# Channel mixing, sphere matrices and sphere convolution as one unrolled stage, ordered by batch entry

## The reference, cut to what matters

```python
x = x + L0_conv(_gn(x), ...)          # attention; its last step is a 1x1 convolution over channels
x = x + L1_conv(_gn(x), weight, bias) # sphere convolution

def _gn(v, G=4, eps=1e-05):           # per batch entry: mean and variance over 2 channels x 256 x 512
    ...
def _L1_conv_ref(x, weight, bias):
    gx, gy = compute_maps(H, W, 3, 3)  # where each of the 9 taps falls on the sphere, constant
    v = bilinear_sample(x, gx, gy)     # 4 neighbours per tap, columns wrap round
    y = einsum('bchwk,ock->bohw', v, w) + bias
```

## Time and profile before

| | |
|---|---|
| median of 3 runs | 1318.74 us (1318.55 to 1319.75) |
| profiled execution | 1318.1 us, span 1315.9 us |
| mean granted clock of TensorE | 0.946 of full |
| busy in the span | PE 1124.3 (85%), VectorE 965.2 (73%), ScalarE 655.0 (50%), GpSimd 820.7 (62%) |
| DMA | 159.28 MB, mean 121 GB/s |

### The profile page before, as it was taken

The page is one execution under the profiler, slowest core; times in us unless marked ns, Lnnn a source line. Parts: engine busy times, 40 slices in busy tenths (PEclk is TensorE's granted clock), DMA queues, the critical chain, the costliest instruction groups (busy, mean ns, idle before and its releaser), DMA issues. The chain is left out here.

```text
span 1315.9 us, 31260 instructions
## 1 busy us (share of the span) xinstructions
PE 1124.3 (85%) x12690; PEld 758.5 (58%) x12690; DVE 965.2 (73%) x1460; ACT 655.0 (50%) x1077; POOL 820.7 (62%) x689
## 2 busy tenths in 40 slices
PE   0399999999883888999999999999994986778997
PEld 0177777777660356666666666666673433434553
DVE  3789899999655998889998998998733881223434
ACT  1555555555430565656666666666662232223456
POOL 0467777777655698888898888888880002890000
PEclk9999999999995789999999999999897997979999
DMA  8824424433367428181717272520005985896621
GB/s 299 249 83 128 120 69 125 118 102 96 64 139 151 73 75 137 36 119 43 138 34 113 51 126 46 107 65 26 18 22 161 339 295 140 190 209 195 202 81 57
DMA packets 138189, 159.28 MB, mean 121 GB/s; under 512 B 19609, under 2 KB 87453, under 8 KB 138057
## 3 DMA queue, kind: packets, MB, share of 16 engines
q1 hardware_dynamic: 113592, 119.37, 38.4%
q10 hardware_dynamic: 15792, 28.81, 6.3%
q0 software_dynamic: 8672, 9.23, 3.3%
HBM read 106.48 MB, written 52.90 MB: 121 GB/s over the span
## 5 line engine op out<-in xcount | busy, mean ns | idle before, releaser
L1126 POOL TENSOR_TENSOR a_pl<-a_prob 128x512 bf16<-128x512 f32 x416 | 452.1, 1113 | 58.1 <-ACT a_prob L1083 54.1
L1083 ACT ACTIVATE a_prob<-a_col 128x512 f32<-128x512 f32 x512 | 303.1, 597 | 190.4 <-PE a_col L973 179.9
L1027 DVE TENSOR_REDUCE a_negmax<-a_row 128x1 f32<-128x512 f32 x512 | 336.9, 693 | 52.4 <-PE a_row L951 52.1
L990 PE MATMUL a_mix<-a_vp,a_prob 128*128 128x65 bf16 x2048 | 196.5, 195 | 1.1 <-DVE a_o L1052 0.9
L990 PEld LDWEIGHTS a_mix<-a_vp,a_prob 128*128 128x128 bf16 x2048 | 164.7, 99 | 54.1 <-issue 6.1
L991 PE MATMUL a_mix<-a_vp,a_pl 128*128 128x65 bf16 x2048 | 194.9, 195 | 0.0
L730 POOL TENSOR_TENSOR f_yl<-f_y,f_yh 128x768 bf16<-128x768 f32 x80 | 132.4, 1674 | 96.6 <-ACT f_yh L677 96.6
L991 PEld LDWEIGHTS a_mix<-a_vp,a_pl 128*128 128x128 bf16 x2048 | 147.5, 99 | 61.8 <-issue 6.3
L677 ACT ACTIVATE f_yh<-f_y 128x768 bf16<-128x768 f32 x80 | 67.4, 844 | 138.9 <-DVE f_y L568 119.7
L951 PE MATMUL a_row<-k,q 96*128 96x512 bf16 x256 | 109.1, 432 | 29.5 <-PEq L222 15.0
L1522 PE MATMUL s_acc<-s_xh,sphere_mat_h 128*104 128x512 bf16 x256 | 103.6, 405 | 35.3 <-DVE s_xl L1489 34.2
(11 more groups left out here) (151 smaller groups left out, 2308.5 us busy)
## 6 DMA issues: line engine op xcount, KB each, us to landing
X<-r_x ACTq DMA_DIRECT2D x16, 526.0 KB, 7.6
q<-in_x SPq DMA_DIRECT2D x8, 1024.0 KB, 7.8
a_v<-V SPq DMA_DIRECT2D x16, 512.0 KB, 4.5
Z<-a_z ACTq DMA_DIRECT2D x32, 256.0 KB, 2.8
r_z<-Z SPq DMA_DIRECT2D x16, 512.0 KB, 8.7
r_x<-in_x SPq DMA_DIRECT2D x32, 256.0 KB, 8.1
s_res<-X SPq DMA_DIRECT2D x38, 208.0 KB
out<-s_y ACTq DMA_DIRECT2D x38, 208.0 KB
```

The lines of the kernel that those rows point to most:

```text
L990: nc.tensor.matmul(mix[h % 2][:, qt, :], ph[p][:, kt, at], vpart, start=kt == 0, stop=False)
L1027: nc.vector.reduce_max(negmax[u][:, QT * h + qt:QT * h + qt + 1], row[row_buffer(h, qt)][:], AX.X, negate=True).then_inc(max_done, 1)
L1083: nc.scalar.activation(prob[head % PROBS][:, kt, :], col[kt % 2][:], ACT.Exp).then_inc(exp_done, 1)
L1126: nc.gpsimd.tensor_tensor(pl[head % PROBS][:, kt, :], prob[head % PROBS][:, kt, :], ph[head % PROBS][:, kt, :], ALU.subtract).then_inc(lo_ ...
```

## The change

`residual` and `sphere` become one function `blend` in one block, without loops: every instruction is written out with constant addresses and constant semaphore values.

- Batch entry 0 is mixed first (8 pairs); makes start with its third pair, two per pair, so 12 of them. Then entry 1's pairs alternate with the rest of the makes and with windows of entry 0: PE does `window(n - 2)` behind pair n, so windows 0 to 5 lie there. The last 4 makes follow, then the other windows.
- The order of windows is that of `places()`: per batch entry ten near windows, the three polar blocks, seven near windows; entry 0 whole, then entry 1.
- Statistics are finished per entry, and scale and offset stay in SBUF: the store and load of S are gone.
- Buffers: z, x and x1 of pairs three deep (four before); raw windows, residuals and y three deep each (one per batch entry before); xn, xh, xl and the window accumulators two deep.
- GpSimd waits until all X1 of an entry is stored, then makes the six copies and the 117 tile loads for this entry alone, entry 0 and then entry 1. The tiles lie in the space of q0 and k0, one set for both entries; a tile is reloaded when entry 0's step on it has been normalised. `normalise` waits for all of an entry's tile loads before its first polar step.
- SP issues the loads of 11 pairs, then per window one raw load, the residual of the window before, and one more pair while there are any. The first raw load of an entry waits for all its X1 stores.
- The last 2 of the weight parts' four subtractions move behind VectorE's first pair; PE waits for the parts before its first make and not before its first pair.

The diff, cut to the new lines that set the order and the buffers (removed lines are left out); the two functions that it removes are printed whole above, and operations not shown here (statistics, makes, wraps, activations) are those of before with other addresses.

```diff
...
+def blend(nc, T, Z, X1, XP, out, mixing, spaces):
...
+        U, RAWS, RES, TWO, ACCS = 3, 3, 3, 2, 3
...
+        MIDDLE = 10
...
+        res = [sb(f"b_res{s}", [M, W]) for s in range(RES)]
+        y = [sb(f"b_y{s}", [M, W]) for s in range(RES)]
+        held = [t[:].bitcast(FP32) for t in spaces]
+        fits = held[0].shape[1] // (W + 1)
+        polar = [held[t // fits][:, t % fits * (W + 1):(t % fits + 1) * (W + 1)] for t in range(TILES)]
...
+            around = [(m, None) for m in range(MIDDLE)] + [(None, m) for m in range(len(SPHERE_POLAR))] + [(m, None) for m in range(MIDDLE, NEARS)]
...
+            def load_pair(g):
+                b, n, s = g // PAIRS, g % PAIRS, g % U
+                if g >= U:
+                    sp.wait_ge(acc_full, 2 * (g - U) + 2)
+                sp.dma_start(z[s][:], Z[b, n * 2 * KR:(n + 1) * 2 * KR].rearrange("(t h) c w -> (h c) t w", t=2)).then_inc(z_in[s], 16)
+                if g >= U:
+                    sp.wait_ge(x1_ready, 2 * (g - U) + 2)
+                for t in range(2):
+                    sp.dma_start(x[s][:, t, :], T["x"][b, :, (2 * n + t) * KR:(2 * n + t + 1) * KR].rearrange("c h w -> h c w")).then_inc(x_in[s], 16)
+            def load_raw(q):
+                b, h0, n, source, index, tiles, entries, step = SEQ[q]
+                if source is None:
+                    return
+                r0, c0, cols = source
+                if index >= RAWS:
+                    sp.wait_ge(xn_done, next(blk[7] for blk in SEQ if blk[4] == index - RAWS) + 1)
+                if index % NEARS == 0:
+                    for s in range(U):
+                        sp.wait_ge(x1_stored[s], stored(b, s))
+                s = index % RAWS
+                sp.dma_start(raw[s][:, 0:cols], X1[b, r0:r0 + KR, :, c0:c0 + cols].rearrange("h c w -> (h c) w")).then_inc(raw_in[s], 16)
+            def load_residual(q):
+                b, h0, n, source, index, tiles, entries, step = SEQ[q]
+                s = q % RES
+                if q >= RES:
+                    sp.wait_ge(y_ready, q - RES + 1)
                 if n == OR:
+                    sp.dma_start(res[s][:], X1[b, h0:h0 + n, :, NEAR:NEAR + W].rearrange("h c w -> c h w")).then_inc(res_in[s], 16)
                 else:
                     for c in range(C):
...
+                        sp.dma_start(res[s][c * OR:c * OR + n], X1[b, h0:h0 + n, c, NEAR:NEAR + W]).then_inc(res_in[s], 16)
...
+            sp.dma_start(bias[:], T["b_sphere"].rearrange("c (a n) -> c a n", a=1).broadcast_to([C, OR, 1])).then_inc(bias_in, 16)
+            for g in range(PAIRS + U):
+                load_pair(g)
+            for q in range(WINDOWS_S + 1):
+                if q < WINDOWS_S:
+                    load_raw(q)
+                if q:
+                    load_residual(q - 1)
+                if PAIRS + U + q < B * PAIRS:
+                    load_pair(PAIRS + U + q)
...
+            for b in range(B):
+                for s in range(U):
+                    pool.wait_ge(x1_stored[s], stored(b, s))
+                for to_row, row, rows in ((0, 0, TOP), (TOP, F - BOTTOM, BOTTOM)):
+                    for to, frm, cols in pieces:
+                        pool.dma_start(XP[b, to_row:to_row + rows, :, to:to + cols].rearrange("h c w -> (h c) w"),
+                                       X1[b, row:row + rows, :, frm:frm + cols].rearrange("h c w -> (h c) w")).then_inc(widened, 16)
+                pool.wait_ge(widened, 16 * 6 * (b + 1))
+                for t, m, k, s, r in polar_loads():
+                    if b and m == 0:
+                        pool.wait_ge(xn_done, step_of_tile(b - 1, t) + 1)
+                    r = r if r < TOP else r - (F - BOTTOM) + TOP
+                    pool.dma_start(polar[t][m * C:(m + k) * C], XP[b, r:r + k, :, PAD_L + s:PAD_L + s + W + 1].rearrange("h c w -> (h c) w")
+                                   ).then_inc(polar_in, 16)
...
+            def pair(b, n):
+                g = PAIRS * b + n
+                pe.wait_ge(z_in[g % U], 16 * (g // U + 1))
+                for t in range(2):
+                    k = 2 * g + t
+                    if k >= ACCS:
+                        pe.wait_ge(x1_ready, k - ACCS + 1)
+                    nc.tensor.matmul(acc[k % ACCS][:], wmix[:], z[g % U][:, t, :], start=True, stop=True).then_inc(acc_full, 1)
...
+            def window(q):
+                b, h0, n, source, index, tiles, entries, step = SEQ[q]
+                pe.wait_ge(mat_lo, makes_for(q))
+                if q >= 2:
+                    pe.wait_ge(y_ready, q - 1)
+                to = acc_s[q % 2][0:M, :]
+                for t, products in enumerate(entries):
+                    s = (step + t) % TWO
+                    pe.wait_ge(xl_done, step + t + 1)
+                    for j, (e, at) in enumerate(products):
+                        first, end = t == j == 0, t == len(entries) - 1 and j == len(products) - 1
+                        nc.tensor.matmul(to, mat_h[:, e, :], xh[s][:, at:at + W], start=first, stop=False)
+                        nc.tensor.matmul(to, mat_h[:, e, :], xl[s][:, at:at + W], start=False, stop=False)
+                        last = nc.tensor.matmul(to, mat_l[:, e, :], xh[s][:, at:at + W], start=False, stop=end)
+                    last.then_inc(used_up, 1)
...
+            for n in range(PAIRS):
+                pair(0, n)
+                if n >= MAKE_FROM:
+                    make(2 * (n - MAKE_FROM))
+                    make(2 * (n - MAKE_FROM) + 1)
+            for n in range(PAIRS):
+                pair(1, n)
+                if n == 1:
+                    group_spread(0)
+                make(2 * (PAIRS - MAKE_FROM + n))
+                make(2 * (PAIRS - MAKE_FROM + n) + 1)
+                if n == 0:
+                    group_sums(0)
+                if n >= 2:
+                    window(n - 2)
+            for k in range(2 * (2 * PAIRS - MAKE_FROM), MAKES):
+                make(k)
+            for q in range(PAIRS - 2, WINDOWS_S):
+                window(q)
+                if q == PAIRS - 2:
+                    group_sums(1)
+                if q == PAIRS:
+                    group_spread(1)
...
+            def finish(q):
+                b, h0, n, source, index, tiles, entries, step = SEQ[q]
+                s = q % RES
+                if q == 0:
+                    v.wait_ge(bias_in, 16)
+                v.wait_ge(used_up, step + len(entries))
+                v.wait_ge(res_in[s], landed(q))
+                if q >= RES:
+                    v.wait_ge(y_stored[s], landed(q - RES))
+                nc.vector.scalar_tensor_tensor(y[s][:], acc_s[q % 2][0:M, :], bias[:], res[s][:], ALU.add, ALU.add).then_inc(y_ready, 1)
...
+            for n in range(PAIRS):
+                add(1, n)
+                if n == 1:
+                    variance(0)
+                if n >= 3:
+                    finish(n - 3)
+                mat_low(2 * (PAIRS - MAKE_FROM + n))
+                mat_low(2 * (PAIRS - MAKE_FROM + n) + 1)
+                if n == 0:
+                    spread(0)
+                if n == 1:
+                    scales(0)
+                if n >= 1:
+                    low(n - 1, SEQ[n - 1][3][2])
+            aggregate(1)
+            for k in range(2 * (2 * PAIRS - MAKE_FROM), MAKES):
+                mat_low(k)
+            finish(PAIRS - 3)
+            for q in range(PAIRS - 1, WINDOWS_S):
...
+            def normalise(q, t):
+                b, h0, n, source, index, tiles, entries, step = SEQ[q]
...
+                if source:
+                    cols = source[2]
+                    frm = raw[index % RAWS][:, 0:cols]
+                    act.wait_ge(raw_in[index % RAWS], 16 * (index // RAWS + 1))
+                else:
+                    cols = W + 1
+                    frm = polar[tiles[t]]
+                    act.wait_ge(polar_in, 16 * LOADS * (b + 1))
+                if k >= TWO:
+                    act.wait_ge(xl_done, k - TWO + 1)
+                nc.scalar.activation(xn[k % TWO][:, 0:cols], frm, ACT.Identity, bias=norm[:, b, 1:2], scale=norm[:, b, 0:1]).then_inc(xn_done, 1)
+                act.wait_ge(xn_done, k + 1)
+                if k >= TWO:
+                    act.wait_ge(used_up, k - TWO + 1)
+                nc.scalar.activation(xh[k % TWO][:, 0:cols], xn[k % TWO][:, 0:cols], ACT.Copy).then_inc(xh_done, 1)
...
+        blend(nc, T, Z, X1, XP, out, mixing, spaces)
```

More of the change, by code:

```diff
@@ L1142, in residual @@
         NB = F // KR
[L1143 to L1161, removed]
@@ L1162, in residual @@
-        KS = 2 * 3 * KR
[L1163 to L1175, removed]
@@ L1192, in matrices @@
[L1192 to L1213, removed]
@@ L1215, in _ @@
[L1215 to L1240, removed]
@@ L1374, in polar_loads, with makes_for, transfers, landed @@
+        SEQ = list(places())
+        WINDOWS_S = len(SEQ)
+        PER_B = WINDOWS_S // B
+        def makes_for(q):
```

(54 more changed lines are left out.)

456 lines of the change are left out of this document (200 added, 256 removed).

## The result

The changed kernel takes **1271.8 us** (median of 4 runs, 1266.7 to 1273.9); in the same comparison the kernel before took 1318.7 us. The ratio is 0.9637, 95% interval 0.9608 to 0.9666: 47 us less, where 25 had been forecast, and just under the low end of the range. The profiled execution took 1271.9 us, its span is 1270.0 us.

The account below looks back on a forecast made before the run. Mixing was taken as near its DMA and VectorE limits, the sphere stage as held by waits on one-deep buffers. Stages summed to 1280.2, plus restart 2.8, interference 3, end 5: span 1291, time 1294 us; range 1272 to 1316.

Parts of the forecast that it names:

- (c): GpSimd's polar copies and 117 loads per entry: entry 0's polar data there at 1144, so PE stands 11 us.
- the restart: After its stall before entry 0's polar blocks, PE restarts at 1.2 GHz, costing 2.8 us.
- The sentence on turns between queues: DMA engines alternate between busy queue rows; with three busy, the six copies' DMA time of about 6 us becomes 18.
- PE bounds it all: Rival: copies take 16 us, or the mixed part ends late and covers the wait; time 1280, range 1272 to 1286, chance 0.17.
- latency stays in charge: Rival: windows run at 4.7 us beside polar loads; all 25 us give 1316, half 1305; range 1302 to 1316, chance 0.20.
- interference (f): Three-deep window buffers beside polar loads: 3 us for the 17 windows that meet them, bounds 0 and 25.
- the tail: End of the kernel, one full window last: about 5 us behind the last matmul.
- (a): Entry 0's mixing, first in the kernel: its X1 stored at 1055 us, bounds 1050 and 1060.
- (b): Entry 1's mixing alternating with windows 0 to 5: window 0 about 1064, end 1120, PE at polar blocks at 1133.
- (d): From 1144.3 on, the remaining near windows and polar steps of both entries: sum 135.9 us, ending at 1280.2.
- The other account: Same forecast in differences: hand-over 13, hidden windows 27, buffer waits 36, tail 2 go; mixing 34, stall 11, restart 5, interference 3 return.
- The slower rival: Copies starve, both entries' polar chains run in sequence on GpSimd; 1331 with copies of 50 and 35; above 1321, chance 0.10.

Follow-up runs that it names:

- mixing first: Changed kernel with all 16 pairs and all makes first, then all 40 windows, none between pairs: 1277.7 us, ratio 0.9689 to the kernel before.

## Why the prediction was wrong

**The step that failed is (c), entry 0's polar data.** It was put at 1144.3 and was there at about 1127, so the stall of 11 us, the first step behind it and the restart did not happen. Four terms were too long. X1 was stored 3.5 us sooner (1051.5 for 1055); the copies took 12.1 and not 20, below even my low bound of 16; the 117 issues took 57.7 and not 62.3; landing 5.6 and not 7. The copies were the largest miss, 7.9 of some 17 us. The bound was wrong in kind: half of the 31.9 us of the old copies supposed that their time goes by bytes, and it went by their form. The sentence on turns between queues made it 18 and missed likewise. The DMA queues over 1056 to 1063 of the kernel after, in which the copies moved:

```profile
q1 hardware_dynamic: 656, 1.22, 53.4%
q0 software_dynamic: 400, 1.17, 49.6%
q10 hardware_dynamic: 11, 0.02, 0.8%
```

Two rows had work there, not three: SyncE's (q1) and GpSimd's (q0) shared the engines about evenly, and ScalarE's (q10) was nearly empty. That agrees with the turns of the Trainium skill, "DMA: Bandwidth & Descriptors", section "Queues, rings and completion order"; the premise of three rows was wrong. And in this form the copies needed 3.5 us of DMA time (0.496 x 7), not 6. So the rival "PE bounds it all" came true, with the mechanism named there (short copies), and was itself 8 us too high. (In "latency stays in charge", half of the 25 us gives 1303 and not 1305, which changes nothing.)

**The sum, term by term.** From 1291.0 to 1270.0: the stall 11.3; the first step's 2.4, which ScalarE and VectorE did beside the last near windows; the restart 2.8, which did not happen (and would have been 1.6); polar steps 2.0, 1.52 us each and not 1.6; interference (f) 2.2 of its 3; the tail 0.7 (4.3 for 5; 6.8 before). That makes 21.4; 0.4 came back before 1133.4. The first three, 16.5 us, follow from step (c).

**What held.** (a) was put 3.5 us too late. (b) had the last make at 1120 (1118.9) and PE at the polar blocks at 1133 (1133.4), but that is in part luck: window 0 began at 1057 and not 1064, and the part then took 62 us and not 56. Rounds took 8.6 to 11.7 us, most of them above the 9 us that I had named as a sign of being wrong, and the late ones waited not for x or z but for raw windows: in the second half, with the DMA engines at 0.81, PE stood 3.3 and 1.9 us behind raw loads for which ScalarE had waited 6.4 and 5.6. So full queues, and PE beside them, held the first half, and late single loads part of the second; data as the limit of the whole, as argued, was not found. (d) had 25.9, 40.1 and 25.9 for the stretches of near windows; measured are 26.3, 40.2 and 26.1. Entry 1's polar data was far ahead: its last issue ended at 1191, where the sum has 1219.

**The other account, 78 us going and 53 coming back.** It must be judged by the experiments. The span of "mixing first" is 40.0 us under that of before, and these are: first y 3.3 sooner, excess 31.8, polar blocks 2.4 (39.6 for 42.0), tail 2.5. Interleaving adds 5.9 of span. So hand-over, hidden windows and the 34 coming back (+13 + 27 - 34 = +6) measured 9 in all. The 36 us of waits were nearly right in size, 31.8, and wrong in cause. By the excess, splitting copies and loads by entry took 9.7 of them (32.9 to 23.2), and the third buffer 12.2 (13.3 to 1.1). Between them lie 9.9 (23.2 to 13.3) that came with the order by entry: entry 1's loads then run partly beside polar blocks, which need no raw windows. That reading of the last part is argued; no run tries it by itself. Nor does any part them from a second cause, that much of entry 0's loads lies beside mixing, before any window. Each excess is from one profiled run, and medians moved by a few us between groups, so these shares are good to some 3 us.

**The slower rival** needed 72 us for both entries' copies; 12 and about 12 were seen (1121.2 to 1133.6). **Latency stays in charge** is refuted by 98% busy PE.

## What to carry to other kernels

Before a transfer's time is scaled by its bytes, look at its shape and at the packets of its queue: an outermost dimension of 2 had made six copies twice as slow as twelve halves. Total waits of an engine are no price: two-deep buffers raised two waits from 35.6 and 2.6 us to 50.7 and 35.4, and cost 7 us. And where a sum puts a resource just late, its neighbour case (just in time) deserves most of its chance: here 11 us of stall were forecast and 1 or 2 us of slack were found, because four terms were each on the short side of what I took.

## What the runs showed of the hardware

SyncE's issues can stretch to several times their length. In the kernel after:

```profile
1055.56 1.25 SPq L1270 DMA_DIRECT2D b_x<-in_x  x2
...
1067.81 5.02 SPq L1270 DMA_DIRECT2D b_x<-in_x  x2
...
1077.76 7.22 SPq L1270 DMA_DIRECT2D b_x<-in_x  x2
```

The same two issues take 1.25 us ahead of GpSimd's row of tile loads (from 1063.6) and 5 to 7 us beside it. In the mixing of the kernel before, at a DMA share of 0.95 but without GpSimd's loads, they took 1.3. GpSimd's loads and full queues are not enough, though: in "mixing first" a pair's x issues beside the tile loads, at a DMA share of 1.06, took 1.62 us. What they wait for the trace does not say. And the issue of a DRAM copy on GpSimd cost 1.27 us in the form over both entries and 0.54 to 0.56 in the form over one (medians), while for the loads into SBUF it was 0.54 and 0.50.
